# An overflow turn of a mixture-of-experts layer that takes one expert and 128 tokens instead of two experts and 64 each

## The chip, the cores and the metric

The kernel runs on one core of a Trainium2 chip. The metric is the device time of one execution in microseconds, lower is better. The engines are PE (TensorE, with PEld for its weight loads), ACT (ScalarE), DVE (VectorE), POOL (GpSimd) and SP (SyncE), which here only issues DMAs. All data is float32.

## The reference

A graph layer and a mixture of experts, each added to its input. N = 1024 nodes, D = 512 features, 16384 edges, 64 experts with 256 hidden features, two experts for each token:

```
x = x + relu(segment_sum(edge_weight * (layernorm(x) @ W)[dst], src) + bias)
m = layernorm(x)                                  # 1024 x 512
w, idx = top_k(sigmoid(m @ Wg.T + bg), 2);  w = w / w.sum()
n = layernorm(m)
for every expert e with its tokens t:             # 2048 (token, expert) places in all
    h1 = (gamma_e * n_t + beta_e) @ W1_e + b1_e   # 512 -> 256
    h3 = (gamma_e * n_t + beta_e) @ W3_e + b3_e
    y_t += w[t, e] * ((silu(h1) * h3) @ W2_e + b2_e)
x = x + y + shared expert of width 32
```

How many tokens an expert gets is known only when the routing has been computed. With the inputs of the reference, the fullest expert gets 78 tokens, the next one 59, and the mean is 32. These counts come from evaluating the routing of the reference on its own inputs.

## The kernel before

**Stages.** First the graph layer: edges are turned into one-hot products and gathered in the tile A, then A is transposed and multiplied with HW (0 to about 170 us). Beside it and after it the routing: for every block of 128 tokens DVE finds the two experts and the rank of each token in its expert's list, and POOL scatters a record of 8 bytes (token, destination row) into `slots` in HBM, at place `expert * LIST + rank` (`LIST` = 1024). `slots` has been filled with a sentinel beforehand: POOL sets a tile to `NOWHERE` (line 401) and SP copies it out (line 296); gathers and scatters skip rows with that index.

**Turns.** Then the experts run in 33 turns. Turns 0 to 31 take two experts each (a pair), the first 64 places (`CAP`) of each list. A turn is: POOL gathers 128 rows into `xg` (line 497); PE transposes them (`turn_rows`, line 1181); DVE multiplies with gamma and adds beta (`rows`, lines 938 and 939); PE computes both hidden layers (`up`, line 1188: 4 chunks of 128 features times 2 experts, 64 weight columns each, 512 output columns); ACT copies them to SBUF (`hidden`, line 619); PE transposes them (`turn_hidden`, line 1197); ACT computes silu (line 626) and DVE the product (line 956), in pieces of 64 tokens since the bias column differs between the two experts; PE multiplies with W2 (`down`, line 1205); ACT copies the result (line 633); POOL scatters it into `totals` (line 501). On PE, turn j stands as: `turn_rows` of j + 1, `up` of j, `down` of j - 1, `turn_hidden` of j.

**The extra turn.** Turn 32 takes chunks of 64 places that lie behind the first 64 of a list. A chunk table made on DVE (`over_table`, `over_experts`) and PE numbers these chunks over all experts; turn 32 takes chunks 0 and 1, one in each half. Were there more than two, a loop behind it (`with pe.If(R2 > 1)`, and the same on the other engines) would run further turns one after the other, without overlap. The expert of each half is known at run time only, so the engines load it into a register first (`over_column`, line 636, on ACT; `over_at_expert`, line 963, on DVE; lines 336, 341 and 347 on SP).

**Weights.** SP keeps six slots of weights ahead of PE: for a pair 2 MB of W1 and W3 (`load_up`, line 303) and 1 MB of W2 (`load_down`, line 306). The weights of the extra turn stand behind those of pair 31 in SP's order: `load_over_up` (line 343), `load_down` of pair 31, `load_over_down` (line 348). Behind the last scatter SP reads `totals` back (line 381), DVE adds (lines 1001 and 1002), SP writes the output (line 384).

Of the kernel before, what the change touches and what calls it, by code (L numbers as in the profile page):

```python
# [10 lines left out]
P = 128  # L11
# [12 lines left out]
LIST = N  # L24
CHUNKS = LIST // CAP
PAIRS = EXPERTS // 2
OVER = 2 * N // CAP
REC = 2
# [7 lines left out]
def moe_gnn(nc, x, src, dst, ew, W, bias, Wg, bg, gamma, beta, W1, b1, W3, b3, W2, b2,  # L36
# [18 lines left out]
    with ctx:  # L55
# [120 lines left out]
        trips = tables[0:1, 144:160]  # L176
        over_at = tables[0:1, 160:192].bitcast(i32)
        over_expert = tables[0:1, 192:224].bitcast(i32)
# [94 lines left out]
        def _(sp):  # L273
# [59 lines left out]
            def load_over(t):  # L333

                for h in range(2):
                    at = sp.value_load(over_at[0:1, ds(2 * t + h, 1)], min_val=0, max_val=EXPERTS * CHUNKS)
                    sp.dma_start(over_list[CAP * h:CAP * h + CAP, :], slots[ds(at * CAP, CAP), :]).then_inc(over_in, 16)

            def load_over_up(t):
                for h in range(2):  # L340
                    e = sp.value_load(over_expert[0:1, ds(2 * t + h, 1)], min_val=0, max_val=EXPERTS - 1)
                    for k, W13v in enumerate((W1v, W3v)):
                        sp.dma_start(of_kind(up_flat[OS], k)[:, h, :], W13v[:, ds(e, 1), :].rearrange("p a n -> p (a n)")).then_inc(w13_in[OS], 16)

            def load_over_down(t):
                for h in range(2):
                    e = sp.value_load(over_expert[0:1, ds(2 * t + h, 1)], min_val=0, max_val=EXPERTS - 1)
                    sp.dma_start(down_flat[OS].rearrange("p (e n) -> p e n", e=2)[:, h, :],
                                 W2v[:, ds(e, 1), :].rearrange("p a n -> p (a n)")).then_inc(w2_in[OS], 16)
# [15 lines left out]
            R2 = sp.value_load(rounds_sb[0:1, 1:2], min_val=1, max_val=OVER // 2)  # L365
# [23 lines left out]
        def _(pool):  # L389
# [128 lines left out]
            R2 = pool.value_load(rounds_sb[0:1, 1:2], min_val=1, max_val=OVER // 2)  # L518
# [11 lines left out]
        def _(act):  # L530
# [104 lines left out]
            def over_column(t):  # L635
                at = [act.value_load(over_expert[0:1, ds(2 * t + h, 1)], min_val=0, max_val=EXPERTS - 1) for h in range(2)]
                return lambda h: ds(at[h], 1)

            for j in range(PAIRS + 1):
# [9 lines left out]
                if j == PAIRS:  # L649
                    act.wait_ge(tokens_ready, 1)  # L650
                    silu(j, j % 2, over_column(0))
# [4 lines left out]
            R2 = act.value_load(rounds_sb[0:1, 1:2], min_val=1, max_val=OVER // 2)  # L656
            with act.If(R2 > 1):
                with act.Fori(1, R2) as t:
                    j = act.snap(t + PAIRS)
                    hidden(j, 0)  # L660
                    column = over_column(t)
                    hold(act)
                    silu(j, 0, column)
# [5 lines left out]
        def _(dve):  # L669
# [229 lines left out]
            link(v.tensor_scalar(passed[:, 0:CHUNKS - 1], steps[:, 0:CHUNKS - 1], count, None, ALU.is_lt))  # L899
            v.tensor_reduce(extra, passed[:, 0:CHUNKS - 1], AX, ALU.add).then_inc(extra_ready, 1)  # L900
# [7 lines left out]
            def over_table():  # L908
# [4 lines left out]
                link(v.tensor_scalar(trips, iota[0:1, 0:OVER // 2], 2.0, first[0:1, 1:2], ALU.mult, ALU.is_lt))  # L913
# [3 lines left out]
                link(v.scalar_tensor_tensor(inside, after, 0.0, inside, ALU.is_ge, ALU.mult))  # L917
                v.scalar_tensor_tensor(chunk, after, expert_at, inside, ALU.add, ALU.mult).then_inc(chunk_ready, 1)

            def over_experts():  # L920
# [3 lines left out]
                link(v.tensor_scalar(over_expert[0:1, :], over_at[0:1, :], 4, None, ALU.arith_shift_right))  # L924
                v.tensor_scalar(over_expert[0:1, :], over_expert[0:1, :], float(EXPERTS - 1), None, ALU.min).then_inc(tokens_ready, 1)

            def over_index(t):

                dve.wait_ge(over_in, t * 32 + 32)
                hold(dve)  # L930
                v.tensor_copy(over_idx, over_list).then_inc(over_ready, 1)
# [9 lines left out]
            def over_rows(j, at):  # L941
# [3 lines left out]
                for h in range(2):  # L945
                    for c in range(DC):
                        ins = v.tensor_scalar(xe[0][:, c, CAP * h:CAP * h + CAP], bank[0][:, c * P + CAP * h:c * P + CAP * h + CAP],
                                              gT[:, c, ds(at[h], 1)], bT[:, c, ds(at[h], 1)], ALU.mult, ALU.add)
# [12 lines left out]

            def over_at_expert(t):
                return [dve.value_load(over_expert[0:1, ds(2 * t + h, 1)], min_val=0, max_val=EXPERTS - 1) for h in range(2)]

            rows(0, 0)
            for j in range(PAIRS + 1):
# [17 lines left out]
                if j == PAIRS:  # L984
                    product(j, j % 2, lambda h: ds(at[h], 1))
                else:
                    product(j, j % 2, lambda h: slice(2 * j + h, 2 * j + h + 1))
            R2 = dve.value_load(rounds_sb[0:1, 1:2], min_val=1, max_val=OVER // 2)
            with dve.If(R2 > 1):
                with dve.Fori(1, R2) as t:  # L990
# [6 lines left out]
                    product(j, 0, lambda h: ds(at_t[h], 1))  # L997
# [7 lines left out]
        def _(pe):  # L1005
# [185 lines left out]

            def turn_hidden(j, b):
# [16 lines left out]
            def down_of(j):  # L1209
# [3 lines left out]
                pe.wait_ge(w2_in[j % SLOTS], 16 * (j // SLOTS + 1) if j < PAIRS else 16 * (PAIRS // SLOTS) + 32)  # L1213
                down(j, j % 2, j % SLOTS)
# [6 lines left out]
            for j in range(PAIRS + 1):  # L1221
# [6 lines left out]
                pe.wait_ge(w13_in[j % SLOTS], 32 * (j // SLOTS + 1) if j < PAIRS else 32 * (PAIRS // SLOTS) + 64)  # L1228
                if j >= 2:
                    pe.wait_ge(h_copied, j - 1)  # L1230
                up(j % 2, j % SLOTS)
# [48 lines left out]
```

## Time and profile before

| | |
|---|---|
| median of 3 runs | 474.7 us (474.32 to 475.35) |
| the profiled execution: its time, its span | 474.9 us, 473.1 us |
| its mean granted TensorE clock | 0.928 |
| PE busy | 403.6 us (85%) |
| DVE, ACT, POOL busy | 200.8, 165.2, 139.9 us |
| moved by DMA | 126.10 MB, mean 267 GB/s |

### The profile page before, as it was taken

Reading aid. Unit: us, or ns where it says so; the run is one execution under the profiler, and the core shown is the slowest. Engines: PE = TensorE matmul, PEld = TensorE weight load, DVE = VectorE, ACT = ScalarE, POOL = GpSimd, SP = SyncE. Lnnn points to the kernel's source line nnn. Section 1 sums busy time; section 2 is a strip of 40 time slices with the busy share of each in tenths; the row PEclk is TensorE's granted clock in tenths of the full one; section 3 lists DMA queues with packets and bytes.
Section 4 is the critical chain, followed back from the end, with each engine's and each line's share of the span. In section 5 each row is a group of like instructions: output and inputs, shape, how many; then the busy total and the mean of one; then the engine's idle time right before and its main releaser. Section 6 shows DMA issues by size and latency. Waiting matters only on the chain.

```text
span 473.1 us, 6490 instructions
## 1 busy us (share of the span) xinstructions
PE 403.6 (85%) x1829; PEld 206.5 (44%) x1830; DVE 200.8 (42%) x663; ACT 165.2 (35%) x406; POOL 139.9 (30%) x228
## 2 busy tenths in 40 slices
PE   2899999999999976599999999988889698897700
PEld 1676666665565543234444434433334333343200
DVE  5866567213757677433332333332131321313036
ACT  9868878332223120033333323332222222222100
POOL 2584344003243453403332233332131311301000
PEclk9989999999999995689999999999899988999765
DMA  4999400010101763259999999999999999997158
GB/s 109 340 402 409 196 0 0 2 40 24 44 23 27 286 184 129 54 193 402 407 403 406 410 405 405 407 407 409 406 408 408 404 407 405 408 399 312 43 201 333
DMA packets 41778, 126.10 MB, mean 267 GB/s; under 512 B 7953, under 2 KB 8529, under 8 KB 41618
## 3 DMA queue, kind: packets, MB, share of 16 engines
q1 hardware_dynamic: 35954, 117.29, 63.9%
q0 software_dynamic: 5792, 8.43, 5.0%
q8 instruction: 14, 0.23, 0.2%
q14 instruction: 18, 0.15, 0.1%
HBM read 121.22 MB, written 13.39 MB: 284 GB/s over the span
## 4 chain that ended last, share of the span: by engine, by line
PE 80%; DVE 5%; DMA 5%; issue 5%; SPq 2%; ACT 1%; ACTq 0%; POOL 0%; DVEq 0%; POOLq 0%
PE bank L1188 28%; PE bank L1205 12%; PE bank L1096 12%; PE bank L1059 7%; PE bank L1066 6%; PE bank L1197 5%; PE bank L1181 3%; PE bank L1056 2%; DMA X<-in_x_dram 2%; PE bank L1084 2%; PE bank L1115 1%; DMA w<-totals 1%; DVE X L1002 1%; DVE X L1001 1%; DMA A<-nx_rows,A 1%
## 5 line engine op out<-in xcount | busy, mean ns | idle before, releaser
L1188 PE MATMUL bank<-w,xhT 128*64 128x512 f32 x368 | 92.5, 649 | 15.1 <-issue 14.2
L956 DVE SCALAR_TENSOR_TENSOR osl<-bank,b13T,osl 128x64 f32<-128x64 f32 x132 | 28.5, 277 | 171.5 <-ACT osl L626 171.4
L619 ACT COPY xh<-bank 128x512 f32<-128x512 f32 x33 | 19.3, 585 | 155.1 <-PE bank L1188 155.1
L1096 PE MATMUL bank<-HW,AT 128*128 128x512 f32 x128 | 57.3, 593 | 0.0
L1188 PEld LDWEIGHTS bank<-w,xhT 128*64 128x64 f32 x368 | 28.7, 147 | 62.3 <-issue 59.8
L1205 PE MATMUL bank<-w,osl 128*64 128x512 f32 x184 | 45.4, 612 | 3.0 <-DVE osl L956 3.0
L501 POOL DMA_INDIRECT totals<-osl,A x17 | 17.3, 1017 | 96.0 <-PE bank L1181 76.4
L540 ACT ACTIVATE osl<-iota,eT 128x128 f32<-128x128 f32 x128 | 39.0, 388 | 12.1 <-PE bank L1059 12.1
L501 POOL DMA_INDIRECT totals<-GW,A x16 | 16.2, 1015 | 85.0 <-PE bank L1181 69.5
L497 POOL DMA_INDIRECT A<-nx_rows,A x33 | 33.8, 1025 | 16.1 <-issue 9.8
L1096 PEld LDWEIGHTS bank<-HW,AT 128*128 128x128 f32 x128 | 23.3, 190 | 23.9 <-issue 23.9
L626 ACT ACTIVATE osl<-bank,b13T 128x64 f32<-128x64 f32 x132 | 30.7, 314 | 3.9 <-PE bank L1197 1.1
L1197 PEld LDWEIGHTS bank<-ident,xh 128*128 128x128 f32 x132 | 18.3, 208 | 26.6 <-issue 26.0
L761 DVE TENSOR_TENSOR A<-A,bank 128x384 f32 x32 | 17.7, 553 | 26.9 <-PE bank L1059 23.6
L1066 PE MATMUL bank<-GW,xhT 128*128 128x512 f32 x64 | 29.0, 596 | 0.0
L1205 PEld LDWEIGHTS bank<-w,osl 128*64 128x64 f32 x184 | 14.6, 141 | 28.8 <-issue 28.8
L1181 PE MATMUL bank<-ident,A 128*128 128x128 f32 x132 | 22.1, 293 | 4.3 <-DMA A<-nx_rows,A 4.3
L1197 PE MATMUL bank<-ident,xh 128*128 128x128 f32 x132 | 24.6, 309 | 0.5 <-ACT xh L619 0.5
L938 DVE TENSOR_TENSOR xhT<-bank,gT 128x512 f32<-128x512 f32 x32 | 21.8, 680 | 5.4 <-PE bank L1181 5.4
L939 DVE TENSOR_TENSOR xhT<-xhT,bT 128x512 f32<-128x512 f32 x32 | 22.2, 694 | 1.1
L1188 PE MATMUL bank<-A,xhT 128*64 128x512 f32 x80 | 20.0, 644 | 2.2 <-issue 2.0
L1188 PE MATMUL bank<-HW,xhT 128*64 128x512 f32 x80 | 20.0, 645 | 2.2 <-issue 2.1
(197 smaller groups left out, 538.9 us busy)
## 6 DMA issues: line engine op xcount, KB each, us to landing
w<-in_L_ffn_W_dram SPq DMA_DIRECT2D x66, 1024.0 KB
A<-in_L_ffn_W_dram SPq DMA_DIRECT2D x15, 1024.0 KB
HW<-in_L_ffn_W_dram SPq DMA_DIRECT2D x10, 1024.0 KB
AT<-in_L_ffn_W_dram SPq DMA_DIRECT2D x5, 1024.0 KB
w<-totals SPq DMA_DIRECT2D x8, 512.0 KB, 7.3
w<-in_L_ffn_W_dram SPq DMA_DIRECT2D x6, 512.0 KB
X<-in_x_dram SPq DMA_DIRECT2D x4, 512.0 KB, 7.1
out_dram<-X SPq DMA_DIRECT2D x8, 256.0 KB, 5.6
```

What stands on the lines that cost most here:

```text
L497: g.indirect_dma_start(xg[b], None, nx_rows, bass.IndirectOffsetOnAxis(ap=index, axis=0), bounds_check=N - 1, oob_is_err=False).then_inc(x ...
L501: g.indirect_dma_start(totals, bass.IndirectOffsetOnAxis(ap=index, axis=0), ysb[b], None, bounds_check=2 * N - 1, oob_is_err=False).then_i ...
L540: ins = a.activation(osl[:, h % 2, k, :], iota[:, :], ACT.Abs, bias=eT[:, 1, ds(j * 32 + 8 * h + k, 1)])
L626: ins = a.activation(sl[b][:, m, CAP * h:CAP * h + CAP], bank[4][:, m * P + CAP * h:m * P + CAP * h + CAP], ACT.Silu, bias=b13T[:, 0, m, c ...
L956: ins = v.scalar_tensor_tensor(hT[b][:, m, CAP * h:CAP * h + CAP], bank[4][:, (HC + m) * P + CAP * h:(HC + m) * P + CAP * h + CAP], b13T[: ...
L1059: ins = t.matmul(bank[q % 4][:, ds(at[k], TW)], osl[:, (q // 2) % 2, (q % 2) * QUAD + k, :], Mq[q % 4][:, k, :], start=False, stop=(k == Q ...
L1066: ins = t.matmul(bank[6 + u][:, :], xhT[:, u, c, :], GW[:, c, :], start=(c == 0), stop=(c == DC - 1))
L1096: ins = t.matmul(bank[4 + s % 2][:, :], AT[:, s % 2, k, :], HW[:, k, :], start=(k == 0), stop=(k == NB - 1))
L1181: ins = t.transpose(bank[b][:, c * P:(c + 1) * P], xg[i][:, c:c + DC * (P - 1) + 1:DC], ident[:, :])
L1188: ins = t.matmul(bank[2 + b][CAP * h:CAP * h + CAP, :], xe[b][:, c, CAP * h:CAP * h + CAP], up_w[v][:, h, :, c, :], start=(c == 0), stop=( ...
L1197: ins = t.transpose(bank[4][:, i * P:(i + 1) * P], hraw[b][:, at:at + HC * (P - 1) + 1:HC], ident[:, :])
L1205: ins = t.matmul(bank[6 + b][CAP * h:CAP * h + CAP, :], hT[b][:, m, CAP * h:CAP * h + CAP], down_w[v][:, h, m, :], start=(m == 0), stop=(m ...
```

## The change

A chunk that an extra turn takes is now 128 places of one expert, instead of two chunks of 64 places of two (possibly different) experts. The first 64 places of each list are taken by the pairs, as before. What follows from it:

- The chunk table counts steps of 128 behind the first 64 places (`STEPS` = 8 of them instead of 15), and a chunk's place in `slots` is 2 times its number plus an offset; the table has one DVE instruction more. There is one extra turn for each chunk instead of one for two.
- A chunk may reach past place 1024 of a list, so lists have 2048 places: `slots` and its sentinel double (from 513 KB to 1025 KB).
- The extra turn's weights are those of one expert: two DMAs of 512 KB (W1, W3) instead of four, one for W2 instead of two, and one list DMA of 128 rows instead of two of 64. SP, ACT and DVE load one expert number instead of two.
- `over_up`, `over_down`: PE multiplies 128 tokens at once, 4 and 2 matmuls in the source with 128 weight columns instead of 8 and 4 with 64. `over_silu`, `over_product`, `over_rows`: 2, 2 and 4 instructions of 128 columns instead of 4, 4 and 8 of 64.
- The 32 pair turns are untouched.

```
-LIST = N
+LIST = 2 * N
+STEPS = N // P
...
             def load_over_up(t):
-                for h in range(2):
-                    e = sp.value_load(over_expert[0:1, ds(2 * t + h, 1)], min_val=0, max_val=EXPERTS - 1)
-                    for k, W13v in enumerate((W1v, W3v)):
-                        sp.dma_start(of_kind(up_flat[OS], k)[:, h, :], W13v[:, ds(e, 1), :].rearrange("p a n -> p (a n)")).then_inc(w13_in[OS], 16)
+                e = sp.value_load(over_expert[0:1, ds(t, 1)], min_val=0, max_val=EXPERTS - 1)
+                for k, W13v in enumerate((W1v, W3v)):
+                    sp.dma_start(of_kind(up_flat[OS], k)[:, 0, :], W13v[:, ds(e, 1), :].rearrange("p a n -> p (a n)")).then_inc(w13_in[OS], 16)
...
+            def over_silu(j, b, t):
+                e = act.value_load(over_expert[0:1, ds(t, 1)], min_val=0, max_val=EXPERTS - 1)
+                act.wait_ge(hT_ps, j + 1)
+                for m in range(HC):
+                    ins = a.activation(sl[b][:, m, :], bank[4][:, m * P:m * P + P], ACT.Silu, bias=b13T[:, 0, m, ds(e, 1)])
+                ins.then_inc(sl_ready, 1)
...
-            mark(v.tensor_scalar(steps[:, 0:CHUNKS - 1], iota[0:64, 1:CHUNKS], float(CAP), None, ALU.mult))
+            mark(v.tensor_scalar(steps[:, 0:STEPS], iota[0:64, 0:STEPS], float(P), float(CAP), ALU.mult, ALU.add))
...
-                link(v.tensor_scalar(trips, iota[0:1, 0:OVER // 2], 2.0, first[0:1, 1:2], ALU.mult, ALU.is_lt))
+                link(v.tensor_scalar(trips, iota[0:1, 0:OVER], first[0:1, 1:2], None, ALU.is_lt))
...
-                link(v.scalar_tensor_tensor(inside, after, 0.0, inside, ALU.is_ge, ALU.mult))
-                v.scalar_tensor_tensor(chunk, after, expert_at, inside, ALU.add, ALU.mult).then_inc(chunk_ready, 1)
+                mark(v.scalar_tensor_tensor(inside, after, 0.0, inside, ALU.is_ge, ALU.mult))
+                link(v.tensor_scalar(chunk, after, 2.0, expert_at, ALU.mult, ALU.add))
+                v.tensor_tensor(chunk, chunk, inside, ALU.mult).then_inc(chunk_ready, 1)
...
+            def over_product(j, b, e):
+                dve.wait_ge(sl_ready, j + 1)
+                for m in range(HC):
+                    ins = v.scalar_tensor_tensor(hT[b][:, m, :], bank[4][:, (HC + m) * P:(HC + m) * P + P], b13T[:, 1, m, ds(e, 1)], sl[b][:, m, :],
+                                                 ALU.add, ALU.mult)
+                ins.then_inc(hT_ready, 1)
...
+            def over_up(b):
+                for c in range(DC):
+                    ins = t.matmul(bank[2 + b][:, :], xe[b][:, c, :], up_w[OS][:, 0, :, c, :], start=(c == 0), stop=(c == DC - 1))
+                ins.then_inc(h_ps, 1)
+            def over_down(j, b):
+                pe.wait_ge(hT_ready, j + 1)
+                for m in range(HC):
+                    ins = t.matmul(bank[6 + b][:, :], hT[b][:, m, :], down_w[OS][:, 0, m, :], start=(m == 0), stop=(m == HC - 1))
+                ins.then_inc(y_ps, 1)
```

SP at the end of its list of weight loads, before the change; `w` are the weight tiles, the lines 341 and 347 load an expert's number:

```order
L303 DMA w<-in_L_ffn_W_dram 128x2x1024 x2
L306 DMA w<-in_L_ffn_W_dram 128x2x1024
L341 TENSOR_LOAD M
L341 ISA x2
L343 ISA
L343 DMA w<-in_L_ffn_W_dram 128x1024 x2
L341 TENSOR_LOAD M
L341 ISA x2
L343 ISA
L343 DMA w<-in_L_ffn_W_dram 128x1024 x2
L306 DMA w<-in_L_ffn_W_dram 128x2x1024
L347 TENSOR_LOAD M
```

The same place after it:

```order
L304 DMA w<-in_L_ffn_W_dram 128x2x1024 x2
L307 DMA w<-in_L_ffn_W_dram 128x2x1024
L340 TENSOR_LOAD M
L340 ISA x2
L342 ISA
L342 DMA w<-in_L_ffn_W_dram 128x1024 x2
L307 DMA w<-in_L_ffn_W_dram 128x2x1024
L345 TENSOR_LOAD M
L345 ISA x2
L346 ISA
L346 DMA w<-in_L_ffn_W_dram 128x1024
```

Between the loads of pair 31's W1 and W3 and its W2, two DMAs of 512 KB are left of four; nothing changed its place.

ACT in the extra turn, before: the copy of turn 31's result, then the two expert numbers, then silu in four pieces and the copy of the extra turn's result:

```order
L633 COPY GW<-bank 128x512
L636 TENSOR_LOAD M
L636 ISA x2
L636 TENSOR_LOAD M
L636 ISA x2
L626 ISA
L626 ACTIVATE osl<-bank,b13T 128x64
L626 ISA
L626 ACTIVATE osl<-bank,b13T 128x64
L626 ISA
L626 ACTIVATE osl<-bank,b13T 128x64
L626 ISA
```

And after:

```order
L631 COPY GW<-bank 128x512
L635 TENSOR_LOAD M
L635 ISA x2
L638 ISA
L638 ACTIVATE osl<-bank,b13T 128x128
L638 ISA
L638 ACTIVATE osl<-bank,b13T 128x128
L631 COPY osl<-bank 128x512
```

One register load and two activations are gone ahead of the copy of the result.

## Rows read from the trace of the kernel before

**Rows 1.** The page: DMA rate in 40 slices, and the group of line 619

```profile
GB/s 109 340 402 409 196 0 0 2 40 24 44 23 27 286 184 129 54 193 402 407 403 406 410 405 405 407 407 409 406 408 408 404 407 405 408 399 312 43 201 333
...
L619 ACT COPY xh<-bank 128x512 f32<-128x512 f32 x33 | 19.3, 585 | 155.1 <-PE bank L1188 155.1
```

**Rows 2.** The chain that ended last, in order: start us, us, what

```profile
324.92 1.97 issue
326.89 3.65 PE bank L1188 x16
...
392.60 1.78 issue
394.39 5.35 PE bank L1188 x16
...
426.03 1.30 issue
427.33 3.65 PE bank L1188 x16
...
433.38 1.88 issue
435.26 5.35 PE bank L1188 x16
...
445.99 3.61 PE bank L1205 x8
451.04 2.24 DMA totals<-osl,A
```

**Rows 3.** Timeline of SP, 404 to 475 us: start, us, engine, line, what

```profile
414.37 5.84 SPq L343 DMA_DIRECT2D w<-in_L_ffn_W_dram  x4
420.26 1.06 SPq L306 DMA_DIRECT2D w<-in_L_ffn_W_dram  x1
422.25 3.06 SPq L348 DMA_DIRECT2D w<-in_L_ffn_W_dram  x2
```

**Rows 4.** Stretches of 1 us: busy time of each engine, PEclk, DMA share, GB/s

```profile
435.00:436.00 1.00, 0.74 (x4) 0.51 (x6) 0.37 (x2) 0.00 (x0) 0.13 (x1) 0.85 0.67 272
...
439.00:440.00 1.00, 1.00 (x7) 0.38 (x5) 0.00 (x0) 0.00 (x0) 0.00 (x0) 0.94 0.26 103
```

**Rows 5.** Timeline, 433 to 446 us

```profile
433.48 0.93 ACT L626 ACTIVATE osl<-bank,b13T 128x64 f32<-128x64 f32 x4
...
442.25 0.75 PE L1197 MATMUL bank<-ident,xh 128*128 128x128 f32 x4
442.42 0.58 ACT L633 COPY GW<-bank 128x512 f32<-128x512 f32 x1 [1.13 <-PE bank L1205]
443.72 1.05 ACT L626 ACTIVATE osl<-bank,b13T 128x64 f32<-128x64 f32 x4 [0.72 <-PE bank L1197]
...
444.99 0.86 DVE L956 SCALAR_TENSOR_TENSOR osl<-bank,b13T,osl 128x64 f32<-128x64 f32 x4 [9.62 <-ACT osl L626]
```

**Rows 6.** Line 636 on ACT's queue: durations min/median/max ns, first and last start

```profile
L636 ACTq TENSOR_LOAD <-M x2: 278/282/287, 442.5 to 443.1; - x2
```

**Rows 7.** Timeline: instructions of 128 columns, or 128 weight columns, in other stages

```profile
105.12 7.03 PE L1096 MATMUL bank<-HW,AT 128*128 128x512 f32 x16
...
36.30 2.43 ACT L540 ACTIVATE osl<-iota,eT 128x128 f32<-128x128 f32 x8
...
22.81 0.85 DVE L777 TENSOR_SCALAR M<-iota,eT 128x128 f32<-128x128 f32 x3
```

**Rows 8.** Timeline, 0 to 32 us: the sentinel and its first reader

```profile
1.72 0.96 POOL L401 MEMSET HW<- 128x1026 f32 x1
...
14.06 0.49 SPq L296 DMA_DIRECT2D slots<-HW  x1
...
29.64 0.59 ACT L552 COPY HW<-bank 128x512 f32 x1
```

**Rows 9.** DMA issues: times, KB each, median us from issue to landing

```profile
slots<-HW SPq DMA_DIRECT2D x1, 513.0 KB, 10.8
```

More of the change, by code:

```diff
@@ L364, in _ @@
             load_over_down(0)
[L365 removed]
+            R2 = sp.value_load(rounds_sb[0:1, 1:2], min_val=1, max_val=OVER)
             with sp.If(R2 > 1):
@@ L650, in _ @@
                     act.wait_ge(tokens_ready, 1)
-                    silu(j, j % 2, over_column(0))
+                    over_silu(j, j % 2, 0)
                 else:
@@ L660, in _ @@
                     hidden(j, 0)
-                    column = over_column(t)
+                    over_silu(j, 0, t)
                     hold(act)
-                    silu(j, 0, column)
                     act.wait_ge(y_out[0], t * 16 + 16 * (PAIRS // YS))
@@ L939, in rows, with over_rows @@
                 v.tensor_tensor(to, to, bT[:, :, 2 * j:2 * j + 2].unsqueeze(3).broadcast_to([P, DC, 2, CAP]), ALU.add).then_inc(xe_ready, 1)
-            def over_rows(j, at):
+            def over_rows(j, e):
                 dve.wait_ge(xe_ps, j + 1)
                 hold(dve)
[L945 to L948, printed above, removed]
+                for c in range(DC):
+                    ins = v.tensor_scalar(xe[0][:, c, :], bank[0][:, c * P:c * P + P], gT[:, c, ds(e, 1)], bT[:, c, ds(e, 1)], ALU.mult, ALU.add)
                 ins.then_inc(xe_ready, 1)
@@ L960, in product @@
                 ins.then_inc(hT_ready, 1)
+            def over_product(j, b, e):
[4 more added lines that the diff above has]
+                ins.then_inc(hT_ready, 1)
             def over_at_expert(t):
-                return [dve.value_load(over_expert[0:1, ds(2 * t + h, 1)], min_val=0, max_val=EXPERTS - 1) for h in range(2)]
+                return dve.value_load(over_expert[0:1, ds(t, 1)], min_val=0, max_val=EXPERTS - 1)
             rows(0, 0)
@@ L996, in _ @@
                     hold(dve)
-                    product(j, 0, lambda h: ds(at_t[h], 1))
+                    over_product(j, 0, at_t)
             for s in range(NB):
@@ L1190, in up @@
                 ins.then_inc(h_ps, 1)
+            def over_up(b):
+                for c in range(DC):
+                    ins = t.matmul(bank[2 + b][:, :], xe[b][:, c, :], up_w[OS][:, 0, :, c, :], start=(c == 0), stop=(c == DC - 1))
[5 more added lines that the diff above has]
+                ins.then_inc(y_ps, 1)
             def turn_hidden(j, b):
@@ L1212, in down_of @@
                     pe.wait_ge(y_ready, j - 1)
-                pe.wait_ge(w2_in[j % SLOTS], 16 * (j // SLOTS + 1) if j < PAIRS else 16 * (PAIRS // SLOTS) + 32)
-                down(j, j % 2, j % SLOTS)
+                pe.wait_ge(w2_in[j % SLOTS], 16 * (j // SLOTS + 1) if j < PAIRS else 16 * (PAIRS // SLOTS) + 16)
+                if j < PAIRS:
+                    down(j, j % 2, j % SLOTS)
+                else:
+                    over_down(j, j % 2)
             pe.wait_ge(z_added, NB)
```

54 lines of the change are left out of this document (26 added, 28 removed).

## The prediction

> **What bounds the kernel now.** I read the page first. Its DMA row says where the limit lies while the turns run: from the 19th to the 36th slice the rate stands at about 400 to 410 GB/s, then falls to 312 and 43 [rows 1]. A pair needs 3 MB of weights, so the weights set the pace there, and PE, though busier than any other engine, waits for them. The same page shows 33 copies of line 619, one for each turn: 32 pairs and one extra turn; the loop for further turns does not run [rows 1].
>
> The chain that ended last is the second view. From 315 us on it has the same pattern again and again: an idle piece of PE named "issue" ahead of a turn's `up`, then the 16 matmul records of `up`. There are eight such pieces of 1.8 to 2.1 us (three are shown: the first, the sixth and the last) and two of 1.3 us. In the chain they are PE waiting for weights, since the other inputs of `up` are ready by then. The last two stand ahead of turn 31 (1.30 us) and of the extra turn 32 (1.88 us, from 433.38 to 435.26 us) [rows 2]. Everything up to the end of the wait for pair 31's weights at 427.33 us is untouched by the change, since SP issues the extra turn's loads behind them: lines 343, 306 and 348 at 414.37, 420.26 and 422.25 us [rows 3]. So the question is what the 46 us from 427.33 us to the end are made of, and which of them the extra turn's shape sets.
>
> The chain also shows TensorE's clock. After six of the eight pieces of 1.8 to 2.1 us `up` took 5.3 us, after two of them 3.65 us, as after both of 1.3 us [rows 2]. In the long ones part of the work ran at 1.2 GHz: the granted clock averages 0.85 in 435 to 436 us and is back at 0.94 in 439 to 440 us [rows 4], with 0.50 between. PE had stood idle ahead of each of these falls. The `down` of turn 32 (3.61 us) is slow as well; PE was idle for 3.0 us ahead of it, from 443.0 to 445.99 us [rows 2, 5].
>
> **The change part by part.**
>
> *The weights of turn 32.* Its W1 and W3 fall from 2 MB to 1 MB. At the 408 GB/s of the slices before [rows 1] the megabyte takes 2.6 us, so the last of it should land at 435.26 - 2.6 = 432.7 us. PE is free at 433.38 us. The wait of 1.88 us goes, and 0.7 us is in hand. What is late next is PE itself: it goes from turn 31's transposes right into `up`. Pair 31's W2 comes behind it, 1 MB, at 435.3 us, and is needed at 437.0; turn 32's W2 by 436.6, needed beyond 441. The DMA share falls from 0.67 to 0.26 between 435 and 440 us while work is left [rows 4], so the 16 DMA engines don't finish together. If it were all engines that had slowed, the megabyte saved would be worth 3.9 us at 272 GB/s, and the data would be there earlier still. Both readings remove the wait.
>
> *The clock in `up` of turn 32.* Without the wait PE has no idle piece between 427.33 us and the end of this `up`. No `up` without such a piece ahead of it is slow in the chain, so I take the fast one. Its 4 matmuls of 128 weight columns write 512 columns each; 8 of the same shape took 7.03 us at line 1096, so 4 take 3.5 us, against 3.65 us for the 8 with 64 columns [rows 2, 7]: two of 64 columns ran side by side before, so halving their number wins nothing. `up` ends at 433.38 + 3.6 = 437.0 instead of 440.61 us. **-3.6 us**, of it 1.88 the wait and 1.7 the clock. Bounds: 0 if the wait is not for these weights; 1.9 if the low clock comes all the same.
>
> *ACT and DVE between `up` and `down`.* First the expert number: `silu` of turn 31 began 0.1 us behind the transposes (433.48 against 433.38 us), that of turn 32 0.7 us behind them (443.72 against 443.0) [rows 2, 5]. Between them stand two register loads that start 0.6 us apart [rows 6]. One is left, and it is done when the copy of line 633 ends. -0.6 us (bounds 0.3, one load's own time, and 0.7). Then `silu`: four pieces of 64 columns took 1.05 us [rows 5]. The trace has no silu of 128 columns; eight activations of 128 columns took 2.43 us [rows 7], so one comes every 0.3 us and two take 0.6 to 0.7 us. -0.37 (bounds 0.1 and 0.5, the latter if width were free and only the number counted). The product: four pieces in 0.86 us [rows 5]; three DVE instructions of 128 columns took 0.85 us [rows 7], so two take 0.6. -0.27 (bounds 0 and 0.4). `over_rows` gets shorter too, but its work was done well ahead of 433 us. Together **-1.24 us**, so `down` starts at 445.99 - 3.6 - 1.24 = 441.15 us.
>
> *The clock in the last `down`.* Its 2 matmuls of 128 columns take what the 4 of 64 took. It ran wholly at the low level: 3.61 us, where half of that, 1.8, is the other level. The idle time ahead of it shrinks from 3.0 to 1.75 us (transposes end at 439.4). That lies just under the eight pieces of which six were followed by a slow `up`, and above the two that weren't. And in such a slow `up` only a part was slow (5.35 instead of 3.65 us, so 1.7 us lost over a span in which clock fell and rose) [rows 2]. Bounds 0 and -1.8; I take **-1.0 us**.
>
> The page "TensorE: Matmul & The Clock Gate" of the Trainium skill (section on what is actually happening) says that the chip's watch over PE's activity runs freely and does not restart with a kernel. By it, where a fall hits the last `down` differs from execution to execution; the rows agree in that idle pieces of one length (1.97 and 1.78 us) have different outcomes. By this rule the term is a draw between its bounds, which leaves the sum as it is.
>
> *Chunk table.* One more DVE instruction of 32 columns at about 201 us, some 0.1 us. PE needs the chunk only behind `up` of turn 0, and DVE is idle afterwards until ACT's silu. Nothing; 0.1 us if that cover were gone. The list DMA and `over_index` run ten turns or more ahead of their use. Nothing either.
>
> *The sentinel.* 513 KB become 1025 KB, and the fill on POOL (0.96 us at 1.72 us) doubles. SP sends it only at 14.06 us, so the fill is hidden. The write landed 10.8 us after its issue, at 24.9 us, and its first reader that waits, the ACT copy of line 552, starts at 29.64 us [rows 8, 9]. The added 512 KB take 1.3 us at 402 GB/s: landed at 26.2, 3.4 us in hand. The other end: if all 10.8 us were the write's own and doubled, it would land at 35.7 us and make ACT 6.1 us late. I take the rate, since much of the 10.8 us is the queue ahead of it: nothing. The prefetched weights come 1.3 us later and are wanted at 200 us.
>
> *The sum*, against the profiled execution: 474.9 - 3.6 - 1.24 - 1.0 = 469.06, so **469.0 us**. The median of the runs is 0.2 us below that execution, which is less than the terms' uncertainty; I keep its time as the base. Behind `down` the way is unchanged: copy, scatter, 2.24 us until it has landed [rows 2], read back, add, write.
>
> **The rivals.**
>
> 1. *The wait goes but the clock falls anyway.* For it: the fall followed six of eight idle pieces, there is still one of 1.30 us ahead of turn 31, and the watch's phase may differ. Against it: both turns behind 1.3 us ran fast. Then `up` still takes 5.3 us and `down` 3.6: 474.9 - 1.88 - 1.24 = 471.8 us; with one of the two fast, about 470.5.
>
> 2. *The change does not reach the chain where I say.* The piece of 1.88 us is named "issue", not DMA; if it ended for another reason (the semaphore of the expert loads is only one of the inputs), nothing of the 3.6 us comes. Against it: 2 MB at 408 GB/s behind the 1 MB of W2 that follows 427.33 us give 427.33 + 7.7 = 435.0 us, where the wait ended. Only the 1.24 us of ACT and DVE are left: 473.7 us.
>
> 3. *Slower: a second extra turn.* Before, one extra turn took two chunks of any experts; now it takes one. With two experts above 64 tokens the loop behind turn 32 would run once, without overlap: load of list and weights, gather, transposes, `up`, silu, `down`, scatter. Turn 32 alone took 18 us from its `up` at 435.26 us to the landing at 453.3 us [rows 2], so the time would be at least 469 + 18 = 487 us. It decides as soon as a second list has a 65th place. The trace can't exclude it, since one extra turn holds one chunk or two; the inputs do: 78 and then 59 tokens. Its chance is what I give to an error in that count.
>
> 4. *The sentinel is late.* With ACT 6.1 us late and nothing absorbed, the gain is used up: 475.1 us. ACT has idle pieces of over 2 us behind 30 us, so the point from which it costs lies at a landing of about 31 us, 5 us later than I expect.
>
> **How the numbers follow.** Forecast, 467.7 to 470.2 us: 0.60. Rival 1, 470.2 to 471.8: 0.24. Rival 2, 472.5 to 473.9: 0.09. Rival 3: 0.02. Rival 4, 471 to 475: 0.05. The lower end is both clock terms at their best (474.9 - 3.6 - 1.24 - 1.8 = 468.3) and 0.6 us for the spread of the runs, 474.32 to 475.35. The range of 8 in 10 takes in the forecast and rival 1: 467.7 to 471.7 us. A change of 0.2% (0.95 us, so below 473.75 us) is about what can be told from none. Faster has the forecast, rival 1 and most of 2 and 4: 0.93; within 0.2%: 0.04; slower 0.03.
>
> **What would show it.** In the profile after: the chain has no idle piece between turn 31's transposes and `up` of turn 32, which starts at about 433.4 us and takes 3.5 to 3.6 us as 8 records at clock 1.00. ACT's silu begins 0.1 us behind the transposes and takes under 0.75 us; the product takes 0.6 us; `down` starts 4.1 to 4.2 us behind the end of `up` instead of 5.4 us, and takes 1.8 to 3.6 us. The turns up to 31 lie where they did, within 0.5 us. DMA moves some 1 MB less (1.5 MB of weights less, 0.5 MB of sentinel more). 34 copies at ACT's line for the hidden layer would mean rival 3; an idle piece of 1.9 us ahead of turn 32 rival 2; a first copy into HW after 30 us rival 4. The prediction is wrong if turn 32's `up` still waits, or if something before 427 us moves.

## The result, and the profile after

| | before | after |
|---|---|---|
| median | 474.51 us (474.14 to 475.35, 4 runs) | 469.6 us (468.86 to 470.63, 4 runs) |
| ratio to before | | 0.9878, 95% interval 0.9846 to 0.9911 |
| the profiled execution: time, span | 474.9, 473.1 us | 469.85, 468.0 us |
| mean granted TensorE clock | 0.928 | 0.941 |
| moved by DMA | 126.10 MB | 125.05 MB |

By the recorded ratio the change makes the kernel 1.2% faster (0.9 to 1.5%). The medians of four runs each differ by 4.9 us, which is 1.0%, and the two profiled spans by 5.1 us. The forecast was 469.0 us.

First the page of after, its DMA row and the group of copies of the hidden layer, which answer to [rows 1]:

```profile
GB/s 110 337 367 410 293 0 0 2 41 24 22 46 25 291 119 197 39 136 390 407 404 408 406 407 405 408 408 405 409 407 405 410 402 408 405 404 322 66 249 293
...
L617 ACT COPY xh<-bank 128x512 f32<-128x512 f32 x33 | 19.3, 585 | 150.8 <-PE bank L1196 148.3
```

There are 33 turns again, and the rate is at the same plateau. The chain of after, from two idle pieces among the last pairs to the scatter of the last turn, answers to [rows 2] (start us, us, what):

```profile
359.20 1.77 issue
360.97 5.35 PE bank L1196 x16
...
417.93 1.76 issue
419.69 3.65 PE bank L1196 x16
...
426.22 1.36 issue
427.58 3.65 PE bank L1196 x16
431.23 1.72 PE bank L1226 x8
432.95 0.68 PE bank L1218 x4
433.62 3.44 PE bank L1203 x8
437.06 1.89 PE bank L1226 x8
441.38 1.97 PE bank L1210 x4
...
444.79 2.24 DMA totals<-osl,A
```

`up` of turn 31 starts at 427.58 us, 0.25 us later than before. From there on the chain differs. The idle piece of 1.88 us ahead of turn 32 is gone: the transposes (line 1218) end and `up` of turn 32 (line 1203) follows, 3.44 us as 8 records instead of 5.35 us as 16. The last `down` (line 1210) starts at 441.38 instead of 445.99 us and takes 1.97 instead of 3.61 us. Between the two `down`s the timeline shows ACT and DVE, and answers to [rows 5]:

```profile
438.86 0.75 PE L1218 MATMUL bank<-ident,xh 128*128 128x128 f32 x4
439.03 0.59 ACT L631 COPY GW<-bank 128x512 f32<-128x512 f32 x1 [1.29 <-PE bank L1226]
439.79 0.63 ACT L638 ACTIVATE osl<-bank,b13T 128x128 f32<-128x128 f32 x2 [0.17 <-PE bank L1218]
...
440.63 0.61 DVE L966 SCALAR_TENSOR_TENSOR osl<-bank,b13T,osl 128x128 f32<-128x128 f32 x2 [5.02 <-ACT osl L638]
441.38 1.95 PE L1210 MATMUL bank<-w,osl 128*128 128x512 f32 x4 [1.77 <-DVE osl L966]
```

The wait of ACT ahead of silu is 0.17 instead of 0.72 us, silu takes 0.63 instead of 1.05 us, the product 0.61 instead of 0.86 us. The clock of the last stretches of 1 us in which PE works (busy time of the engines, then granted clock, DMA share, GB/s):

```profile
433.00:434.00 1.00, 1.00 (x6) 0.76 (x7) 0.00 (x0) 0.86 (x3) 0.00 (x0) 1.00 0.47 193
437.00:438.00 1.00, 1.00 (x7) 0.43 (x8) 0.00 (x0) 0.58 (x1) 0.00 (x0) 1.00 0.00 0
441.00:442.00 1.00, 0.61 (x2) 0.41 (x3) 0.24 (x1) 0.00 (x0) 0.37 (x1) 1.00 0.08 33
```

It stands at 1.00 throughout. Before, it was 0.50 in most of `up` (435.26 to 440.61 us) and of `down` (445.99 to 449.6 us) of turn 32, between the stretches of [rows 4]:

```profile
436.00:437.00 1.00, 1.00 (x4) 0.30 (x2) 0.00 (x0) 0.00 (x0) 0.00 (x0) 0.50 0.57 230
...
446.00:447.00 1.00, 1.00 (x4) 0.42 (x6) 0.00 (x0) 0.00 (x0) 0.00 (x0) 0.50 0.00 0
```

The weights are all in SBUF by 437 us (DMA share 0.00) instead of 440.

The budget: `down` starts 4.61 us earlier (although `up` of turn 31 starts 0.25 us later) and is 1.64 us shorter, together 6.25 us. The span is only 5.1 us shorter; the rest, 1.15 us, lies behind the last scatter, where SP reads `totals` back and writes the output. That stretch took 19.6 us before and 20.7 us after, though its instructions are the same.

### The profile page after: what moved, and what is told of

The parts are those of the page before. It is cut to its first block, busy times and chain, and to the rows that moved or that the text cites. A ratio compares the mean times of both kernels' runs of the same rounds, so it can differ in the third digit from the quotient of the medians.

```text
span 468.0 us, 6425 instructions
## 1 busy us (share of the span) xinstructions
PE 401.1 (86%) x1817; PEld 206.0 (44%) x1818; DVE 199.6 (43%) x658; ACT 164.8 (35%) x404; POOL 141.3 (30%) x228
## 2 busy tenths in 40 slices
DMA packets 41330, 125.05 MB, mean 267 GB/s; under 512 B 7889, under 2 KB 8465, under 8 KB 41042
## 4 chain that ended last, share of the span: by engine, by line
PE 82%; DMA 5%; issue 5%; DVE 4%; SPq 3%; ACT 0%; ACTq 0%; DVEq 0%; POOLq 0%
PE bank L1196 27%; PE bank L1226 12%; PE bank L1104 12%; PE bank L1067 7%; PE bank L1074 6%; PE bank L1218 5%; PE bank L1189 3%; DMA w<-totals 2%; DMA X<-in_x_dram 2%; PE bank L1064 2%; PE bank L1148 2%; PE bank L1092 2%; PE bank L1123 1%; PE bank L1203 1%; PE bank L1050 1%
## 5 line engine op out<-in xcount | busy, mean ns | idle before, releaser
L1196 PE MATMUL bank<-w,xhT 128*64 128x512 f32 x352 | 89.2, 652 | 13.4 <-issue 12.8
L956 DVE SCALAR_TENSOR_TENSOR osl<-bank,b13T,osl 128x64 f32<-128x64 f32 x128 | 27.5, 277 | 163.6 <-ACT osl L624 163.6
L1196 PEld LDWEIGHTS bank<-w,xhT 128*64 128x64 f32 x352 | 27.5, 148 | 59.4 <-issue 57.0
L1226 PE MATMUL bank<-w,osl 128*64 128x512 f32 x176 | 41.8, 593 | 0.0
L624 ACT ACTIVATE osl<-bank,b13T 128x64 f32<-128x64 f32 x128 | 29.6, 314 | 3.2 <-PE bank L1218 0.4
L1226 PEld LDWEIGHTS bank<-w,osl 128*64 128x64 f32 x176 | 13.5, 137 | 24.4 <-issue 24.4
L1189 PEld LDWEIGHTS bank<-ident,A 128*128 128x128 f32 x132 | 19.2, 211 | 4.2 <-DMA A<-nx_rows,A 4.2
```

What stands on the lines that cost most here:

```text
L624: ins = a.activation(sl[b][:, m, CAP * h:CAP * h + CAP], bank[4][:, m * P + CAP * h:m * P + CAP * h + CAP], ACT.Silu, bias=b13T[:, 0, m, c ...
L956: ins = v.scalar_tensor_tensor(hT[b][:, m, CAP * h:CAP * h + CAP], bank[4][:, (HC + m) * P + CAP * h:(HC + m) * P + CAP * h + CAP], b13T[: ...
L1189: ins = t.transpose(bank[b][:, c * P:(c + 1) * P], xg[i][:, c:c + DC * (P - 1) + 1:DC], ident[:, :])
L1196: ins = t.matmul(bank[2 + b][CAP * h:CAP * h + CAP, :], xe[b][:, c, CAP * h:CAP * h + CAP], up_w[v][:, h, :, c, :], start=(c == 0), stop=( ...
L1226: ins = t.matmul(bank[6 + b][CAP * h:CAP * h + CAP, :], hT[b][:, m, CAP * h:CAP * h + CAP], down_w[v][:, h, m, :], start=(m == 0), stop=(m ...
```

## The experiments

The kernels stand in three groups: the first four, the next four and the last three of the table. Times of one group share a chip and the runs of the kernel before; times of different groups are compared by their ratio to before. A gain in us below is (1 - ratio) times before's median; the difference of two medians can differ from it by up to 0.8 us. The idle pieces and the times beside them are of one profile for each kernel.

| kernel | median us (runs) | ratio to before, 95% interval | idle ahead of `up` 32, its time | idle ahead of last `down`, its time | reading back to the end |
|---|---|---|---|---|---|
| weights_only | 472.27 (12) | 0.9918 (0.9888 to 0.9948) | none, 3.58 | 3.00, 3.45 | 19.4 |
| shapes_only | 474.17 (12) | 0.9968 (0.9939 to 0.9997) | 1.91, 5.37 | 1.77, 3.00 | 19.4 |
| lists_1024 | 471.02 (9) | 0.9912 (0.9879 to 0.9945) | none, 3.44 | 1.77, 1.97 | 20.4 |
| after_again | 469.67 (6) | 0.9887 (0.9844 to 0.9930) | none, 3.44 | 1.77, 1.97 | 19.8 |
| second_trip | 491.89 (4) | 1.0334 (1.0275 to 1.0393) | | | |
| sentinel_x3 | 468.69 (2) | 0.9854 (0.9786 to 0.9922) | none, 3.44 | 1.77, 1.97 | 20.4 |
| before_pe_busy | 473.54 (12) | 0.9948 (0.9919 to 0.9976) | 1.95, 5.35 | 0.32, 1.95 | 19.6 |
| after_more_idle | 470.78 (10) | 0.9903 (0.9872 to 0.9935) | none, 3.44 | 2.81, 3.09 | 20.5 |
| after_pe_busy | 470.07 (6) | 0.9863 (0.9825 to 0.9901) | none, 3.44 | 0.20, 1.97 | 19.6 |
| after_third | 469.36 (6) | 0.9855 (0.9814 to 0.9897) | none, 3.44 | 1.78, 1.97 | 20.4 |
| before_again | 477.31 (8) | 1.0014 (0.9980 to 1.0048) | 1.96, 5.29 | 2.99, 3.37 | 20.0 |

Before's own medians in the three groups were 475.76, 476.2 and 476.13 us. In second_trip `up` of turn 32 took 3.44 us with no idle piece ahead of it, and its `down` took 1.97 us behind 1.78 us.

### Only the weights: weights_only

The kernel before, with this edit and the waits of PE lowered to match (a second expert, if there were one, would be computed with wrong weights; here that half holds no token):

```
             def load_over_up(t):
-                for h in range(2):
+                for h in range(1):
...
             def load_over_down(t):
-                for h in range(2):
+                for h in range(1):
```

Expected:

> The kernel before with one part of the change: only the first expert's weights of the extra turn are loaded (W1, W3: 1 MB instead of 2; W2: 0.5 instead of 1). The second half of the turn, which holds no token here, multiplies with what lies in the slot. Theory (the wait of PE for those weights and the low clock behind it are the first term): `up` of turn 32 follows the transposes at about 433.4 us with no idle piece, the 1.24 us of ACT and DVE stay, the idle piece ahead of the last `down` stays at 3 us. 3.6 us faster than before, about 470.9 us. Rival (the idle piece of 1.88 us is not for these weights, the gain comes from the shapes on ACT, DVE and PE): within 0.5 us of before. Second rival (wait goes, low clock comes anyway): 1.9 us faster, 472.6 us.

Measured: 0.9918, which is 3.9 us less than before (2.5 to 5.3), where 3.6 was expected; the medians differ by 3.5 us. The rival that gives all the gain to the shapes is out, and so is the one by which the low clock comes anyway, at 1.9 us. The chain of this kernel:

```profile
427.49 1.35 issue
428.84 3.65 PE bank L1188 x16
432.49 1.72 PE bank L1205 x8
434.21 0.68 PE bank L1197 x4
434.88 3.58 PE bank L1188 x16
438.47 1.74 PE bank L1205 x8
...
443.86 3.45 PE bank L1205 x8
```

`up` of turn 32 follows the transposes and is fast, with the old shapes; the last `down` is still slow behind 3.00 us of idle PE.

### Only the shapes: shapes_only

The kernel after, with the weights loaded twice (W2 in the same way as W1 and W3, and PE's waits raised to match):

```
             def load_over_up(t):
                 e = sp.value_load(over_expert[0:1, ds(t, 1)], min_val=0, max_val=EXPERTS - 1)
-                for k, W13v in enumerate((W1v, W3v)):
-                    sp.dma_start(of_kind(up_flat[OS], k)[:, 0, :], ...).then_inc(w13_in[OS], 16)
+                for h in range(2):
+                    for k, W13v in enumerate((W1v, W3v)):
+                        sp.dma_start(of_kind(up_flat[OS], k)[:, h, :], ...).then_inc(w13_in[OS], 16)
```

Expected:

> The kernel after, but a second copy of the expert's W1, W3 and W2 is loaded beside the first and waited for, as much as before: 2 MB and 1 MB. Theory: the idle piece of about 1.9 us ahead of `up` of turn 32 is back, mostly with the low clock behind it (5.2 us for `up`); what is left of the gain is 1.2 us on ACT and DVE and 0 to 1.8 us on the last `down`: 1.2 to 3 us faster than before, about 472.5 us. Rival (shapes make the gain): as after, 469.6 us.

Measured: 0.9968, 1.5 us less than before (0.1 to 2.9), where 1.2 to 3 was expected. In its chain the idle piece and the slow `up` are back:

```profile
435.59 1.91 issue
437.50 5.37 PE bank L1205 x8
442.87 1.89 PE bank L1228 x8
...
447.19 3.00 PE bank L1212 x4
```

So 128 weight columns alone do nothing for the slow `up` (5.37 us here, 5.35 us with 64), and the piece named "issue" is the wait for the weights: putting the bytes back puts it back. The two halves of the change add up within what the runs can tell: 3.9 + 1.5 = 5.4 us, and the whole change in the same group gives (1 - 0.9887) x 475.76 = 5.4 us (3.3 to 7.4). That they agree so closely is chance: by the medians it is 3.5 + 1.6 = 5.1 against 6.1 us.

### The larger lists: lists_1024

```
-LIST = 2 * N
+LIST = N
...
-                link(v.tensor_scalar(over_expert[0:1, :], over_at[0:1, :], 5, None, ALU.arith_shift_right))
+                link(v.tensor_scalar(over_expert[0:1, :], over_at[0:1, :], 4, None, ALU.arith_shift_right))
```

Expected:

> The kernel after with lists of 1024 places again (sentinel 513 KB). Theory: the added sentinel is hidden, so the time is that of after within 0.3 us, 469.6 us, and the first copy into HW lies where it lay or up to 0.8 us earlier. Rival (the larger sentinel delays the first stage and costs part of the gain): 0.5 to 1 us faster than after.

Measured: 0.9912 against 0.9887 for after in the same group. The median is 471.02 us, 1.35 us above that of after, where at most 0.3 was expected; the intervals (0.9879 to 0.9945 and 0.9844 to 0.9930) overlap, and what difference there is has the sign against the rival. The times are too coarse to exclude a cost of 0.5 to 1 us by themselves. The trace of after says more: ACT's first copy into HW has no idle time ahead of it there, so ACT did not wait for the larger sentinel:

```profile
30.43 0.57 ACT L550 COPY HW<-bank 128x512 f32 x1
```

### After once more: after_again

Expected:

> The kernel after, unchanged, on the same chip as the other three. 469.6 us within 0.5. Of interest beside its time: whether the last `down` is fast (1.95 us) again, and whether the reading back of totals to the end takes 20.7 us again or 19.6 as in the trace of before. Theory (chance): between these values. Rival (the change lengthens it): 20.7 again here and in all kernels with the new shapes.

Measured: 469.67 us, the last `down` fast again, and the reading back 19.8 us, between the two.

### The price of a second trip: second_trip

```
-                v.tensor_scalar(rounds_sb[0:1, 1:2], n_trips, 1.0, None, ALU.max)
+                v.tensor_scalar(rounds_sb[0:1, 1:2], n_trips, 2.0, None, ALU.max)
```

Expected:

> The kernel after, with the number of extra turns raised from 1 to 2: the loop behind turn 32 runs once, with a list that holds only sentinels (no token), as a second expert with more than 64 tokens would make it run. It prices rival 3 of the prediction. Theory: list, expert number and weights are loaded one after the other behind turn 32 and nothing overlaps: at least 18 us more than after, about 488 us; with the list's landing (about 12 us when the queue is full, less when it is empty) up to 495 us. Rival (the loads run ahead while turn 32 finishes, so only PE, ACT and DVE count): under 12 us more, below 482 us.

Measured: 491.89 us, 1.0334 of before, and 22.3 us over the 469.6 us of after (medians of different groups). The timeline shows the steps:

```profile
444.97 0.35 SPq L337 DMA_DIRECT2D A<-slots  x1
...
449.25 0.17 DVE L933 CAST A<-A 128x2 int32<-128x2 f32 x1 [7.31 <-DMA totals<-osl,A]
450.30 1.05 POOL L495 DMA_INDIRECT A<-nx_rows,A  x1 [3.83 <-DVE A L933]
453.02 1.10 PE L1189 MATMUL bank<-ident,A 128*128 128x128 f32 x4 [8.98 <-DMA A<-nx_rows,A]
...
455.99 5.87 PE L1203 MATMUL bank<-w,xhT 128*128 128x512 f32 x8 [1.87 <-DVE xhT L948]
...
464.83 1.98 PE L1210 MATMUL bank<-w,osl 128*128 128x512 f32 x4 [1.54 <-DVE osl L966]
...
468.29 1.00 POOL L499 DMA_INDIRECT totals<-osl,A  x1 [16.94 <-ACT osl L631]
```

DVE takes up the list only once the scatter of turn 32 has landed; from one scatter to the next it is 22.8 us. The theory had the weights in this chain, too, and there the timeline says otherwise: SP issues list and weights at 444.97 to 448.2 us, before that scatter has landed (445.49 + 3.54 = 449.03 us), and `up` waits for DVE (1.87 us), not for weights. The rival is out by its time (under 12 us more), though it was right that the loads run ahead. What costs is the rest of the chain, and in it the clock: `up` takes 5.87 us where that of turn 32 takes 3.44. The list held no token here, so this is the price of an empty trip. With two experts above 64 tokens the kernel before would need no such trip, and the change would cost about 15.7 us (491.89 against 476.2 us) instead of giving 5.

### The slack of the sentinel: sentinel_x3

The same tile is also written to two further tensors, and ACT and POOL wait for all three:

```
+            for a in more_slots:
+                sp.dma_start(a.rearrange("(p n) r -> p (n r)", p=P), sentinel).then_inc(sentinel_out, 16)
...
-                act.wait_ge(sentinel_out, 16)
+                act.wait_ge(sentinel_out, 48)
```

Expected:

> The kernel after, with the sentinel written to two more tensors of the same size that nobody reads, and all three waited for by the copy into HW and by POOL: 2 MB more, 5.1 us at 408 GB/s. It measures the slack of rival 4. Theory (the first stage absorbs some of it): the sentinel lands at about 32 us, the first copy into HW at 32 instead of 30.4 us, and since ACT has idle pieces of 2 us there, PE's stage ends less than 1 us later; time within 1 us of after. Rival (ACT has no slack): 2 us or more slower than after.

Measured: 468.69 us, a ratio of 0.9854. These are 2 runs with an interval of 0.9786 to 0.9922, whose upper end is 2.1 us above after (0.9878), so the time alone doesn't exclude the rival's 2 us. The timeline of ACT:

```profile
27.91 1.06 ACT L544 ACTIVATE osl<-osl 128x1024 f32<-128x1024 f32 x1
31.95 0.59 ACT L553 COPY HW<-bank 128x512 f32 x1 [2.98 <-DMA more_slots<-HW]
32.43 0.59 ACT L548 COPY xhT<-bank 128x512 f32<-128x512 f32 x1
32.91 2.45 ACT L541 ACTIVATE osl<-iota,eT 128x128 f32<-128x128 f32 x8
```

Here ACT does wait for the writes, 2.98 us, and then goes on without the idle piece it had behind this copy (2.14 us). In after the copy came at 30.43 us, here at 31.95; but PE's next stage, with its first 16 records of HW times A, starts at 96.75 us here and at 98.31 us in after. With 2 MB more than the change adds, the wait appears and is absorbed.

### What makes the last `down` slow: before_pe_busy and after_more_idle

PE of the kernel before gets work in its wait:

```
+            for _ in range(12):
+                t.matmul(bank[5][:, 0:P], ident[:, :], ones[:, :], start=True, stop=True)
             down_of(PAIRS)
```

Expected:

> The kernel before, with 12 matmuls of 128 columns into a free bank between the transposes and the `down` of turn 32, where PE waited for 3 us; each takes about 0.21 us, so they fill 2.5 us of the wait. The output is unchanged. Theory (the low clock of the last `down` comes from the idle time ahead of it): `down` takes 1.9 to 2.0 us instead of 3.6 and the clock stays at 1.00 there; 1.1 us faster than before on average (0 to 1.7 in one run). Rival (the clock falls for another reason, such as the slow `up` before it): `down` is slow again in the profile and the time that of before.

In the kernel after, ACT gets four more silu instructions ahead of its two:

```
+                for i in range(more):
+                    a.activation(hraw[1][:, P * i:P * i + P], bank[4][:, 0:P], ACT.Silu, bias=b13T[:, 0, 0, ds(e, 1)])
                 for m in range(HC):
```

Expected:

> The kernel after, with 4 more silu instructions on ACT (written to a free tile) ahead of those of turn 32: they make PE's wait ahead of the last `down` 1.2 us longer, 3.0 instead of 1.8 us, which is what it was before. The output is unchanged. Theory (length of the idle piece decides the clock of the last `down`): `down` takes 3 to 3.6 us again; 1.2 + about 1 = 2.2 us slower than after. Rival (the `down` was slow before because it followed a slow `up`): `down` stays at 1.95 us, 1.2 us slower than after.

PE of before_pe_busy (timeline):

```profile
442.12 0.74 PE L1197 MATMUL bank<-ident,xh 128*128 128x128 f32 x4
442.70 2.84 PE L1241 MATMUL bank<-ones,ident 128*128 128x128 f32 x24
445.86 1.94 PE L1205 MATMUL bank<-w,osl 128*64 128x512 f32 x8 [0.32 <-DVE osl L956]
```

```profile
446.00:447.00 1.00, 1.00 (x6) 0.41 (x6) 0.00 (x0) 0.00 (x0) 0.00 (x0) 1.00 0.00 0
```

`down` takes 1.94 instead of 3.59 us at clock 1.00, though a slow `up` of 5.35 us stands before it. And after_more_idle, PE and a stretch in the middle of its `down`, with granted clock 0.50:

```profile
441.69 3.07 PE L1212 MATMUL bank<-w,osl 128*128 128x512 f32 x4 [2.81 <-DVE osl L968]
```

```profile
443.00:444.00 1.00, 1.00 (x3) 0.19 (x1) 0.00 (x0) 0.00 (x0) 0.00 (x0) 0.50 0.07 16
```

With 2.81 us of idle PE instead of 1.77 the `down` is slow behind a fast `up`. Both rivals fall as sole causes: a slow `up` ahead isn't enough to make the `down` slow, and isn't needed. In times: before_pe_busy gains 2.5 us on before (1.1 to 3.9) where 1.1 was expected and 1.65 is what its `down` shows; after_more_idle is 2.1 us over the one other kernel of its group with the new shapes and no more idle time or turns (468.69 us, 2 runs), 2.2 expected, but the intervals of these two overlap, so the profile carries this reading. shapes_only bounds the rule: its `down` stood behind 1.77 us of idle PE, as in after, and was slow in part (3.00 us). Of 2.8 to 3.0 us all four were followed by a slow `down`, of 1.77 or 1.78 us one of seven. That one, shapes_only, is also the only one of the seven with a wait and a slow `up` in the same turn; whether these lowered the clock again isn't tested, and one case doesn't show it.

The pieces ahead of the `up`s, counted over the 13 profiles from about 315 us on, say the same with more cases. Behind 32 pieces of 0.5 to 1.48 us no `up` was slow (3.65 us each). Behind 42 pieces of 1.75 to 1.86 us 16 were slow (5.29 us or more), behind 60 pieces of 1.87 to 2.38 us 46 were (5.09 us or more). So the clock falls more often behind longer pieces, but the length doesn't tell whether it does in one case.

### Filling the last gap, and the reading back: after_pe_busy, after_third, before_again

after_pe_busy is the kernel after with 7 such matmuls ahead of the last `down`; the other two are the kernels after and before, unchanged.

> The kernel after, with 7 matmuls of 128 columns into a free bank between the transposes and the `down` of turn 32; at 0.21 us each they fill 1.5 of the 1.8 us in which PE waits there. The output is unchanged. Theory (the idle piece decides the clock of that `down`, and in some executions of after it still falls there): 0.3 to 0.6 us faster than after on average, 469.2 us; `down` takes 1.95 us. Rival (with 1.8 us idle the clock no longer falls there in any execution): the time of after.

> The kernel after, unchanged, beside the other two on one chip. 469.6 us within 1. In question is the reading back: from SP's first read of totals to the end it took 20.7, 19.8, 20.4, 20.5 and 20.4 us in five kernels with the whole change, 19.4 to 19.6 in four without. If that is a mark of the change, this one shows 20 or more; if it is chance, it may show 19.5.

> The kernel before, unchanged, for a second profile of it. Theory (the two slow pieces, `up` and `down` of turn 32, come from idle PE ahead of them): the wait ahead of `up` of turn 32 is again 1.8 to 2.0 us, `down` is slow again, at least in part. The reading back takes 19.4 to 19.6 us if the longer one is a mark of the change, up to 20.7 us if it is chance.

after_pe_busy has 0.9863, after 0.9855 in the same group: no gain is seen, and the `down` is as fast without the filler. That fits the rival; but each interval is 0.004 (1.8 us) to either side, so a gain of 0.3 to 0.6 us isn't excluded, and that the clock falls there in no execution can't be shown by the few that were profiled. No kernel of the study beats after beyond its interval.

The reading back took 19.6 us in after_pe_busy, which has the whole change, and 20.0 us in before_again. So it is not fixed by the change: 19.4 to 20.0 us in five profiles without all of it, 19.6 to 20.7 us in seven with the new shapes and the smaller weights (second_trip left out). The two ranges overlap, but their means (19.6 and 20.3 us) differ; whether 0.6 us of it belongs to the change, and by what path, stays open. before_again repeats the two slow pieces (1.96 us idle, then 5.29; 2.99 us idle, then 3.37).

## Why the prediction was right

**The weights of turn 32: right, and the largest part.** The wait of 1.88 us went, PE went straight into `up`, and SP's last weights were in by 437 us, as worked out (436.6). weights_only shows that the bytes do it, shapes_only that the shapes without the smaller load don't.

**The clock in that `up`: right.** The 1.7 us that the low clock had cost left with the wait. Term: -3.6 us; `up` ended at 437.06 us in the chain, forecast 437.0, with a start of turn 31 that was 0.25 us later. So the term measured 3.8 us.

**Two tiles of 64 columns against one of 128: right.** 3.44 us against 3.58 us for `up`, both at 1.00, 3.5 forecast.

**ACT and DVE: right in sum and parts.** Register load 0.55 (0.6 forecast), silu 0.42 (0.37), product 0.25 (0.27): 1.22 us against 1.24. The costs of 128-column instructions taken from other stages [rows 7] held for silu, too. The chain has 1.06 us (4.32 us from the end of `up` to the last `down`, 5.38 before), because a piece was missing from the sum: `down` of turn 31 took 1.89 instead of 1.73 us. It follows an `up` of 128 weight columns now, and has 64 itself. shapes_only shows the same 1.89, weights_only 1.74. The weight loads (PEld) of this `down` show where it comes from, first in weights_only, then in after:

```profile
437.87 0.14 PEld L1205 LDWEIGHTS bank<-w,osl 128*64 128x64 f32 x2 [0.29 <-issue]
```

```profile
436.99 0.20 PEld L1226 LDWEIGHTS bank<-w,osl 128*64 128x64 f32 x4 [0.76 <-issue]
```

In weights_only the first load runs 0.59 us before `up` ends (438.46 us), in after only 0.07 us before its end (437.06 us). The page "TensorEngine Tiling (Array Packing)" of the Trainium skill (Key Properties) has a rule for this, that a change of the tiling mode drains TensorE. The trace agrees: the loads wait for the end of `up`, and 0.16 us is the price here. It takes back what the merged `up` had won: from the start of `up` of turn 32 to the end of this `down` it is 3.44 + 1.89 = 5.33 us in after and 3.58 + 1.74 = 5.32 us in weights_only.

**The clock in the last `down`: right in kind, too small in size.** Forecast -1.0 between 0 and -1.8, measured -1.64 in the profile of after, and 1.97 us for this `down` in the chain of all six profiles that have the new shapes and the smaller weights and nothing added around it (after, after_again, after_third, lists_1024, sentinel_x3, second_trip). The prediction also called the term a draw between its bounds; the six came out alike. The step took the eight idle pieces of 1.8 to 2.1 us as its measure, of which six were slow. The idle piece was 1.77 us. That is the short end of those eight, and counted over all 13 profiles only 5 of 20 `up`s behind pieces of 1.75 to 1.79 us were slow; so the term, sized by six of eight, was too small. (The two pieces that the prediction calls one length, 1.97 and 1.78 us, aren't; there the longer one was followed by the fast `up`.) The outcome of pieces of this length differs by place: ahead of an `up` of the same trace 1.76 us was followed by a fast one, 1.77 us (at 359.20) by a slow one. So -1.64 in the profile was the likely outcome and not a certain one.

**What hid the miss.** The reading back was 1.15 us longer in the profile of after than in that of before; the prediction had it unchanged. 469.06 - 0.64 (`down`) - 0.2 (`up`) + 0.18 (ACT, DVE and the drain) + 0.25 (start) + 1.15 = 469.8 us, which is the time of the profiled execution (469.85). So that 469.0 comes so near is in part luck: 0.84 us more than forecast was gained, and 1.58 us of other things lost. How much of the 1.15 us is chance is open: the same kernel gave 19.8 and 20.4 us later (after_again, after_third).

**Sentinel and chunk table: right.** The sentinel landed 12.7 us after its issue at 14.38 us, so at 27.1 us (26.2 forecast), before ACT's first copy into HW:

```profile
slots<-HW SPq DMA_DIRECT2D x1, 1025.0 KB, 12.7
```

That copy came at 30.43 us. I had named "a first copy into HW after 30 us" as the sign of rival 4, and that sign was badly chosen: in lists_1024, with the small sentinel, it came at 31.33 us, for PE's sake. The start of this stage moves by itself, and the releaser beside the copy is what tells; in sentinel_x3 it names the DMA.

**The rivals.** 1 (clock falls anyway) did not occur in any profile with the whole change. 2 (only 1.24 us) is excluded by weights_only. 3 was priced at 487 us or more and measured at 491.89. 4 did not occur: ACT's copy waits in neither after nor lists_1024 for the sentinel, and with 2 MB on top of the change its wait of 2.98 us was absorbed.

## What to carry to other kernels

Where transfers set the pace, ask which bytes lie ahead of the last step and whether they carry data: a half turn of empty places cost a megabyte of W1 and W3, some 2.6 us of transfer and 1.88 us of PE's wait, and with it the clock. A short idle piece on PE can cost as much again through the low clock behind it, so a term for a removed wait has two parts. Packing one expert instead of two into an extra turn pays only as long as it doesn't add a turn that runs without overlap: that price (22 us) is more than four times the gain.

## What the runs showed of the hardware

- The longer PE has been idle, the more often the clock is low in what follows: behind pieces of up to 1.48 us in none of 32 cases, of 1.75 to 1.86 us in 16 of 42, of 1.87 to 2.38 us in 46 of 60, of 2.8 to 3.0 us (ahead of `down`) in 4 of 4. 24 matmul records of filler in a wait of 3 us kept the clock at 1.00, and 1.65 us came back (one profile; 2.5 us on the ratio, 1.1 to 3.9); they cost PE nothing that anyone waited for.
- One matmul of 128 weight columns takes as long as two of 64 columns that run side by side (3.44 against 3.58 us for `up`), so merging them gains only the 0.14 us.
- Going from a matmul of 128 weight columns to a pair of 64 columns cost 0.16 us, as much as the merging had won.
- The time of one kernel varies by execution and chip (before: 471.57 to 478.63 us over 16 runs on one chip), and much of it arises ahead of the change: `up` of turn 31 starts between 426.05 and 430.52 us in the profiles. From there to the start of the last `down` it is 13.80, 13.80 and 13.81 us in the three profiles of after, and 18.66 and 18.68 us in the two of before. The slow `down` itself (3.61 and 3.37 us) and the reading back repeat less well.
